# Half of a layer norm on ScalarE, one later row of maxima, and rows turned by a product

## What is computed

```python
x = _layernorm(x + _L0_attn_ref(x, ...))         # linear attention, 16 heads
x = _layernorm(x + _L0_xattn_ref(x, ctx, ...))   # causal self-attention + cross-attention
x = _layernorm(x + _L0_ffn_ref(x, ...))          # one of 8 experts for each token

# the second layer, T=512 queries, 1024 context rows, H=16 heads of D=16
q, k, v = _heads(x @ Wq + bq), _heads(x @ Wk + bk), _heads(x @ Wv + bv)
att = jnp.where(causal, jnp.einsum('bhqd,bhkd->bhqk', q, k) * scale, -jnp.inf)
y = jnp.einsum('bhqk,bhkd->bhqd', softmax(att), v)
qc, kc, vc = _heads(x @ Wcq + bcq), _heads(ctx @ Wck + bck), _heads(ctx @ Wcv + bcv)
y = y + jnp.einsum('bhqk,bhkd->bhqd', softmax(jnp.einsum('bhqd,bhkd->bhqk', qc, kc) * scale), vc)
```

## Time and profile before

| | us |
|---|---|
| median of 3 runs | 2242.48 (2242.23 to 2243.74) |
| profiled execution | 2242.68 |
| its span, first to last instruction | 2240.8 |
| outside the span | 1.9 |

### The profile page before, as it was taken

How to read it: one execution, slowest core, us unless ns; L and a number is a source line. 1 busy time by engine, 2 the same in 40 slices (tenths; PEclk the granted TensorE clock), 3 DMA queues, 4 the chain that set the end, 5 groups by cost and what they waited for, 6 DMA issues and landing times. The chain is left out here.

```text
span 2240.8 us, 51067 instructions
## 1 busy us (share of the span) xinstructions
PE 2155.1 (96%) x16290; PEld 1349.3 (60%) x16291; DVE 1364.8 (61%) x3905; ACT 1100.7 (49%) x1680; POOL 367.4 (16%) x628
## 2 busy tenths in 40 slices
PE   8999999999999999999999999999999999799998
PEld 4555555556455555555555555565556455599997
DVE  2588358844784468645883588358844785354454
ACT  1267525761477237722774267525762477233332
POOL 1011111111111111111111111111111111122222
PEclk9999999999999999999999999999999999899999
DMA  7440035102610162005400450035102610755553
GB/s 239 158 167 25 1 110 204 47 2 86 226 49 2 65 224 72 2 11 208 141 2 11 153 173 25 1 108 204 48 2 86 226 49 1 245 186 179 177 182 110
DMA packets 115762, 235.74 MB, mean 105 GB/s; under 512 B 19614, under 2 KB 42655, under 8 KB 113344
## 3 DMA queue, kind: packets, MB, share of 16 engines
q1 hardware_dynamic: 112112, 224.23, 29.9%
q0 software_dynamic: 3408, 8.41, 1.0%
HBM read 154.04 MB, written 73.17 MB: 101 GB/s over the span
## 5 line engine op out<-in xcount | busy, mean ns | idle before, releaser
L1221 ACT ACTIVATE es<-ps 128x1024 f32<-128x1024 f32 (+1 forms) x704 | 665.0, 984 | 241.4 <-PE ps L826 178.7
L1432 DVE TENSOR_REDUCE craw<-ps 128x1 f32<-128x512 f32 x1024 | 636.0, 683 | 95.7 <-PE ps L790 93.9
L790 PE MATMUL ps<-hk,hq 64*128 64x512 f32 x1024 | 382.6, 449 | 13.3 <-DVE craw L1428 5.6
L824 PE MATMUL ps<-hq,hk 64*128 64x512 f32 x1024 | 323.1, 436 | 2.2 <-ACT es L1221 2.2
L826 PE MATMUL ps<-mrow,minus 64*128 64x512 f32 x1024 | 285.6, 390 | 0.0
L1428 DVE CUSTOM_DVE_ANT_0 ps<-ps,causal 128x512 f32<-128x512 f32 (+3 forms) x512 | 235.7, 519 | 74.7 <-PE ps L787 74.3
L790 PEld LDWEIGHTS ps<-hk,hq 64*128 64x128 f32 x1024 | 173.8, 184 | 177.3 <-DVE craw L1432 119.1
L856 PE MATMUL ps<-es,vca 128*17 128x256 f32 x4096 | 276.7, 382 | 1.1
L678 POOL TENSOR_SCALAR_AFFINE_SELECT es<-es 128x256 f32<-128x256 f32 x256 | 99.0, 406 | 619.6 <-ACT es L1221 619.4
L1751 ACT ACTIVATE hT<-ph,b1s 128x128 f32<-128x128 f32 x312 | 89.0, 368 | 183.3 <-PE ph L1714 183.3
L826 PEld LDWEIGHTS ps<-mrow,minus 64*128 64x128 f32 x1024 | 165.4, 185 | 10.6
(11 more groups left out here) (210 smaller groups left out, 2833.4 us busy)
## 6 DMA issues: line engine op xcount, KB each, us to landing
w1s<-in_w1T SPq DMA_DIRECT2D x39, 1024.0 KB, 5.4
hk<-scr_kc SPq DMA_DIRECT2D x64, 512.0 KB, 5.1
scr_kc<-staged SPq DMA_DIRECT2D x16, 1024.0 KB, 4.2
scr_qc<-staged SPq DMA_DIRECT2D x32, 512.0 KB, 4.5
scr_q<-staged SPq DMA_DIRECT2D x32, 512.0 KB, 5.3
hq<-scr_qc SPq DMA_DIRECT2D x56, 256.0 KB, 4.5
hq<-scr_q SPq DMA_DIRECT2D x56, 256.0 KB, 4.2
hk<-scr_k SPq DMA_DIRECT2D x56, 256.0 KB, 4.6
```

The lines of the kernel that those rows point to most:

```text
L790: last = mm(pb, hq[i][at, T + t * P:T + (t + 1) * P], hk[i][at, T + half * BANK:T + (half + 1) * BANK], start=True, stop=True)
L824: mm(pb[a], hk[i][rows[a], T + j * P:T + (j + 1) * P], hq[i][rows[a], T:2 * T], start=True, stop=False)
L1221: nc.scalar.activation(es[:, k % ERING, :].rearrange("p (a c) -> p a c", a=HB)[:, :, 0:w], eslot[k % 2][:].rearrange("p (a c) -> p a c", a ...
L1432: last = v.reduce_max(craw[p % 2][:, t, a:a + 1, 1 + half], pb, AX.X)
```

## The change

Three parts, all in the loop:

1. The layer norm behind the linear attention: VectorE computes `lnb = -mean/sqrt(var)` (one more instruction on 128x4) and writes tiles 0 and 1 of `x1`; ScalarE writes tiles 2 and 3 as `r_s*scale + lnb` in two activations. TensorE and GpSimd wait for both. The read-out of `kc1` moves behind the copies of `x1a` and `x1b` on both engines.
2. The unit `row` of the last pair stands behind the two `weigh` units that followed it.
3. A `row` is a matmul of `mpad` by an identity in fp32r instead of a transpose in fp32. One copy of the identity to fp32r is made at the start.

```diff
+CLEARED = [job[0] for job in JOBS if job[0] != "kc1"]
+CLEARED.insert(CLEARED.index("x1b") + 1, "kc1")
@@ heads_order
+        order += take(0, True)
         order += take(1)
         if k < steps:
             order.append(("exp", *divmod(k, NU)))
         order += take(HB)
         if k + 1 < steps:
             order.append(("exp", *divmod(k + 1, NU)))
-        order += take(1, True)
+        order += take(1)
         order += [("weigh", *divmod(m, NU)) for m in late]
@@ pool
                 pool.wait_ge(s_ln, cur(b, 2, 1))
+                pool.sem_inc(s_past, 1)
+                pool.wait_ge(s_lnact, b + 1)
@@ tensor, maxima_rows
-                tr(pb[:, 0:P], mpad[:], ident[:]).then_inc(s_ring, 1)
+                mm(pb[:, 0:P], mpad[:], ident_r[:], start=True, stop=True).then_inc(s_ring, 1)
@@ tensor
                 pe.wait_ge(s_ln, cur(b, 2, 1))
+                pe.sem_inc(s_pace, 1)
+                pe.wait_ge(s_lnact, b + 1)
@@ scalar
+                act.wait_ge(s_stat, b + 1)
+                for i in range(NT // 2, NT):
+                    last = nc.scalar.activation(x1[:, i, 0:C], r_s[:, i, :], ACT.Identity, bias=lnb[:, i:i + 1],
+                                                scale=nwt[:, LN_AT, i:i + 1])
+                last.then_inc(s_lnact, 1)
+                nc.scalar.activation(x1T[:, 0, :], full("x1a"), ACT.Copy).then_inc(s_act, 1)
                 high_part("kc1", 1, 1, TC_)
-                nc.scalar.activation(x1T[:, 0, :], full("x1a"), ACT.Copy).then_inc(s_act, 1)
@@ vector
-                layer_norm()
-
+                layer_norm((lnb, s_stat))
+
+                v.tensor_copy(x1T[:, 1, :], full("x1b")).then_inc(s_dve, 1)
                 low_part("kc1", 1, 1, TC_)
-                v.tensor_copy(x1T[:, 1, :], full("x1b")).then_inc(s_dve, 1)
@@ layer_norm_steps
+    if shared is not None:
+        lnb, s_stat = shared
+        v.scalar_tensor_tensor(lnb[:], mv[:, 0, :], -1.0, y0, ALU.mult, ALU.mult).then_inc(s_stat, 1)
+        n //= 2
```

More of the change, by code:

```diff
@@ L36 @@
 LN_EPS = 1e-5
+LN_AT = 3
 STAB = 1e-6
@@ L68 @@
 HALF = {"x1a": 0, "x1b": 1, "qc1": 0, "q1": 1, "proj0": 0, "proj1": 1}
-ACT_AT = {name: sum(who in "AB" for _, who, _, _ in JOBS[:n + 1]) for name, n in JN.items()}
-DVE_AT = {name: sum(who in "DB" for _, who, _, _ in JOBS[:n + 1]) for name, n in JN.items()}
+CLEARED = [job[0] for job in JOBS if job[0] != "kc1"]
+CLEARED.insert(CLEARED.index("x1b") + 1, "kc1")
+ACT_AT = {name: sum(WHO[f] in "AB" for f in CLEARED[:n + 1]) for n, name in enumerate(CLEARED)}
+DVE_AT = {name: sum(WHO[f] in "DB" for f in CLEARED[:n + 1]) for n, name in enumerate(CLEARED)}
 N_ACT, N_DVE = ACT_AT["kf3"], DVE_AT["kf3"]
@@ L267, in attentions @@
         mrow = [sb(f"mrow{i}", [P, T], F32R) for i in range(2)]
-        mpad = sb("mpad", [P, P])
+        mpad = sb("mpad", [P, P], F32R)
         zt = sb("zt", [P, 2 * NT * HB, VW])
@@ L334, in attentions @@
         nwi = sb("nwi", [P, 2, NT], I32)
+        lnb = sb("lnb", [P, NT])
         x1 = sb("x1", [P, NT, CR])
@@ L342, in attentions @@
         inblock = sb("inblock", [P, NT])
+        ident_r = sb("ident_r", [P, P], F32R)
         zk = sb("zk", [P, 2, T // 2])
@@ L407, in attentions @@
         s_ln = sem("s_ln")
+        s_stat = sem("s_stat")
+        s_lnact = sem("s_lnact")
         s_st = {n: sem(f"s_st_{n}") for n in STAGED}
@@ L1288, in _ @@
             v.memset(blank, 0.0)
-            v.memset(mpad[:], 0.0)
+            v.memset(mpad[:].bitcast(F32), 0.0)
             v.memset(ksbd[:], 0.0)
@@ L1313, in _ @@
             v.tensor_copy(tri[:], y_s[:, 0, 0:P])
+            v.tensor_copy(ident_r[:], ident[:])
             v.tensor_copy(upto[:, 0:B * NT], iota[:])
@@ L1398, in residual, with layer_norm @@
                     step(last)
-                def layer_norm():
-                    layer_norm_steps(v, step, r_s, x1[:, :, 0:C], stats, mv, nwt, nwi, s_ln)
+                def layer_norm(shared=None):
+                    layer_norm_steps(v, step, r_s, x1[:, :, 0:C], stats, mv, nwt, nwi, s_ln, shared=shared)
                 dve.wait_ge(s_xb, cur(b, 2, 1))
@@ L1528, in _, with layer_norm_steps @@
             assert steps[0] == NSTEP, steps[0]
-def layer_norm_steps(v, step, src, dst, stats, mv, nwt, nwi, done, n=NT):
+def layer_norm_steps(v, step, src, dst, stats, mv, nwt, nwi, done, n=NT, shared=None):
     even, odd = stats[:, :, 1:3], stats[:, :, 4:6]
```

## The result

| | before | after |
|---|---|---|
| median, us | 2243.47 (2242.23 to 2243.99, 7 runs) | 2250.21 (2248.21 to 2251.34, 7 runs) |
| span of the profiled execution | 2240.8 | 2248.7 |
| mean granted clock | 0.994 | 0.993 |

The ratio is 1.0031 with a 95% interval of 1.0019 to 1.0042: the changed kernel is **slower by 6.7 us**. The forecast was 2244.4, no measurable change, with a range up to 2249.0. The time lies outside of it. The forecast started from 2242.68, and the kernel before came out 0.8 us higher in this measurement (2243.47). So of the 5.8 us between forecast and result, 5.0 belong to the change (+6.7 instead of +1.7) and 0.8 to the starting point.

What follows compares the result with a forecast made beforehand. TensorE, busy 96% of the span, was taken as the bound, with ScalarE setting the pace past the last row. Shared norm +5.0, last row -3.3 and one-pass row 0 gave +1.7 on 2242.68: 2244.4 us, range 2238.0 to 2249.0.

Steps and rivals of the forecast that it cites:

- transposes, a turn: Behind the first layer norm: TensorE's transposes start at 91.56 instead of 91.84, 0.28 us earlier in each turn.
- ScalarE's tile / the pair: Shared layer norm: one 128x256 activation on ScalarE takes 0.49 us, two overlapping by 0.10 take 0.88.
- S: Start of the transposes behind the layer norm in a turn: 91.84 before, forecast 91.56 after; later steps count from it.
- near copies of `qc0`, issue: Four copies of `qc0` ahead of the first maxima: 3.33 us to issue behind the store of `kc1`, instead of 2.43.
- first maxima: TensorE's first maxima in a turn: start at S + 10.03 instead of S + 9.13, 0.62 us later in each turn.
- last row, a turn: Last `row` of a turn, moved behind weighted sums: next exponential 0.42 us earlier, 0.41 a turn, -3.3 us in all.
- row's product / in all: One-pass fp32r product for a row: 326 ns, the saved pass spent on slower weight loads, 0 us in all.
- Term 1, the shared norm: Layer norm shared with ScalarE and `kc1` moved back: first maxima 0.62 us later a turn, +5.0 us in all.
- The hand-over: From `k0`'s last low part, done at S + 9.9, to TensorE's first maxima, not before S + 10.0.
- the two paths: What holds the first maxima: `kc1`'s store through `q0` and `k0`, S + 10.0; near copies of `qc0`, S + 10.03.
- The slower rival: At the first maxima: near copies of `qc0` collide harder with `kc1`'s store, +6.3 us, 2249.0; chance 0.15.

Runs made afterwards that it cites:

- three engines: Changed kernel with q0 in its own place and v's second part ahead, norm tiles two on VectorE, one on ScalarE, one on GpSimd: 2242.68 us, 1.0000.

## Where the prediction held and where it failed

| step | predicted | measured |
|---|---|---|
| transposes, a turn | -0.28 | -0.10 |
| ScalarE's tile / the pair | 0.49 / 0.88 | 0.59 / 1.09 |
| store of `kc1` issued | S + 3.77 | S + 3.76 |
| `q0` high starts | S + 7.76 | S + 7.83 |
| near copies of `qc0`, issue | 3.33 | 2.86 |
| first maxima | S + 10.03 | S + 10.19 |
| clock behind the wait | not priced | +2.6 in all |
| last row, a turn | -0.41 | -0.43 (alone: -0.42) |
| row's product / in all | 326 ns / 0 | 322 ns / 0 |
| sum, against the kernel before | +1.7 | +6.7 |
| time | 2244.4 | 2250.2 |

**What held.** That `kc1` going back costs more than the shared norm gives, and by which way: store, landing, `q0` high, two low parts, each within 0.1 us. That the idle time moves to the maxima and grows to some 1.6 us (1.71). That the row gives ScalarE's 0.32 us of idle time plus the overlap and not TensorE's 0.85. That the saved pass goes into the weights: the load takes 186 ns. The Trainium skill ("TensorE: Matmul & The Clock Gate", section "Weight-path perf modes — Fast Weight Load (FWL) and DoubleRow") turns the fast load on for 128 weights of a type other than FP32, with four times as its figure for fp8 and no win for fp32. For fp32r the trace shows no fast load, 186 ns against some 140 ns for the fp32 weights of the transposes, and the product alone gave nothing.

**Term 1, the shared norm, was mis-sized: +5.0 predicted, +7.5 measured** (8.3 - 0.8). Two pieces make the 2.5. The tile: I built 0.49 from activations that read PSUM, of which none had a scale for each row, and it measured 0.593, inside its bounds of 0.40 and 0.69. That took 0.18 us of the 0.28 from each turn, 1.4 in all. The kernel before does have a row with such a scale, ScalarE's four parts of `mrow` (columns as in the earlier trace rows):

```profile
L1213 ACT ACTIVATE mrow<-ps,inblock 128x128 fp32r<-128x128 f32 x256 | 73.3, 383 | 0.0
```

Plain copies take 0.40 us for 256 columns and 0.60 for 512, so one of 128 would take 0.30, and the scale costs some 0.08 (an estimate). With the bias and the scale the tile comes to 0.57 and the transposes to 0.12 earlier, close to the measured 0.10. This term could have been had from the rows.

The hand-over: I had the last low part end at S + 9.9 and let TensorE start 0.1 behind it. It ended at S + 9.96, and the row starts 0.23 us behind it (101.07 + 1.41 = 102.48, then 102.71). With both the maxima came 1.03 us later behind the transposes on the mean of the turns, not 0.90, 1.1 in all. I had taken the near copies for the later path, with 3.33 us from a place where two stores of 512 KB are ahead. Behind one store of 1 MB they take 2.86, so that path gives S + 9.6, as the kernel with `q0` in its own place shows. All of it is the second of the four copies, 1.02 us instead of 0.59. Whether the size of the stores or the time between them and the copies makes the difference to 3.33 is open. That the two paths stood at the same time in the forecast hid that one of them was wrong by 0.4 us.

**The step left out is the clock.** I wrote that TensorE's idle time "moves from the layer norm to the maxima and grows", and went on as if only the idle time itself cost something. TensorE was then idle 1.7 us at one place, and in 2 of 8 turns the granted clock fell behind it, for 1.3 us each. Neither a term nor a rival held this. Without it the sum would be +4.1, which I would have had to call no measurable change. With the clock priced and the rest as it was, the forecast would have come out at +4.3, 2247.0, and with the term of the shared norm right and no clock at 2246.9. So neither of the two alone puts the kernel outside of the range, also with the starting point 0.8 higher; together they do.

**The slower rival** named the right side and nearly the size (2249.0), but by a harder collision of the near copies, and they collided less, 2.86 us instead of 3.33. That its number came close is luck. It said that it decides from maxima 1.0 us later than now. Against the kernel before, turn by turn, they were 0.9 to 1.0 us later, by the other path.

## What to carry to other kernels

Work taken from one engine to shorten a wait pushes back what the other engine did meanwhile, so follow that work to its last waiter: here through a store and a shared staging place to maxima that start 0.9 us a turn later. When a forecast makes one idle stretch of TensorE longer, price the clock behind it as well. Before moving work between engines look for work that can fill the wait as it is: moving the second part of `v` ahead of it was worth 12.1 us on the changed kernel, 2.6 of them the fallen clock, and needs only a count and the place of one wait.

## What was not expected of the hardware

- **The clock behind waits of like length.** TensorE idle for 1.1 to 1.24 us at one place: no fall behind it in the 8 turns of any kernel's profiled execution. Idle for 1.67 to 1.73 us: 2 of 8 turns in the changed kernel, 2 of 8 with `kc1` late, 1 of 8 with one tile on GpSimd, 0 of 8 with three engines. Idle for 8.35 us: 8 of 8. What decides between turns with the same wait stays open; no run here separated it.
- **ScalarE from SBUF with a bias and a scale for each row:** 593 ns for 128x256, against 400 ns from PSUM without them. By the rows above, bias and scale account for some 0.17 us of the 0.19 (an estimate), which leaves little for reading from SBUF; no run changed one of them alone.
- **GpSimd on the same tile:** 1.38 us, with two scalars for each row. VectorE makes four in that time, one after the other with some overlap.
- **Small copies behind a store:** four of 64 KB take 2.43 us to issue with nothing large ahead, 2.86 when a store of 1 MB in one DMA was issued 1.25 us ahead, and 3.33 behind two of 512 KB, the second issued 0.7 us ahead.
